# Attention probabilities kept in four places instead of two, with the value products of two chunks issued back to back in every second chunk

## The reference

```python
Q = query @ Wq + bq
K = key @ Wk + bk
V = value @ Wv + bv
scores = jnp.einsum('bhqd,bhkd->bhqk', Q, K) / jnp.sqrt(jnp.float32(HEAD_DIM))
attn = jax.nn.softmax(scores, axis=-1)
ctx = jnp.einsum('bhqk,bhkd->bhqd', attn, V)
```

## Time and profile before

| what | us |
|---|---|
| three timed executions | 533.49, 533.64, 536.86 |
| median | 533.64 |
| span of the profiled execution, first to last instruction | 538.0 |

### The profile page before, as it was taken

One profiled execution on the slowest core, in us unless ns is written; L12 is line 12 of the kernel. 1 busy time (PEld: TensorE's weight loads), 2 busy tenths in 40 slices (PEclk: granted clock), 3 DMA queues, 4 the chain that ended last, 5 costly groups with the idle time before them and its releaser, 6 DMA issues.

```text
span 538.0 us, 10079 instructions
## 1 busy us (share of the span) xinstructions
PE 431.0 (80%) x3977; PEld 249.1 (46%) x3977; DVE 376.2 (70%) x979; ACT 263.5 (49%) x452; POOL 86.3 (16%) x101
## 2 busy tenths in 40 slices
PE   3998877766788878400787899999899899989997
PEld 1344433334556665100233456566566566644444
DVE  7456999999566695885685988889788784271112
ACT  4264888765422393100102456566566567634443
POOL 2000000000100003677891000210210210200000
PEclk9999999989999999755788999999999999999999
DMA  8500266422641202882270003474383382000000
GB/s 287 214 2 0 94 201 186 130 86 86 196 115 57 59 2 66 214 192 85 60 155 18 1 1 76 100 174 94 81 174 78 98 256 60 3 0 1 0 0 17
DMA packets 28718, 50.05 MB, mean 93 GB/s; under 512 B 2464, under 2 KB 18400, under 8 KB 28672
## 3 DMA queue, kind: packets, MB, share of 16 engines
q1 hardware_dynamic: 26848, 45.74, 31.4%
q0 software_dynamic: 1536, 3.67, 2.7%
q10 hardware_dynamic: 288, 0.00, 0.0%
HBM read 39.96 MB, written 9.45 MB: 92 GB/s over the span
## 4 chain that ended last, share of the span: by engine, by line
PE 43%; DVE 37%; issue 8%; POOL 6%; ACT 3%; DMA 2%; DVEq 0%; POOLq 0%
PE banks L1586 7%; PE banks L1562 7%; POOL arena L544 6%; PE banks L1617 5%; DVE arena L1206 5%; DVE mx L1009 4%; DVE work L1235 4%; PE banks L1664 4%; PE banks L1678 4%; DVE arena L1259 2%; PE banks L1292 2%; DVE mx L1017 2%; PE banks L1430 2%; PE banks L1296 2%; DVE work L1201 2%
## 5 line engine op out<-in xcount | busy, mean ns | idle before, releaser
L1009 DVE TENSOR_REDUCE mx<-banks 112x1 f32<-112x500 f32 x168 | 106.9, 675 | 20.2 <-PE banks L1562 20.2
L771 ACT ACTIVATE arena<-banks 128x896 f32<-128x896 f32 x96 | 87.9, 917 | 51.9 <-PE banks L1617 51.2
L1314 PE MATMUL banks<-steps,one 128*128 128x500 f16 (+1 forms) x201 | 56.5, 377 | 32.3 <-DVE hcol L957 32.3
L1586 PE MATMUL banks<-arena 128*32 128x112 f32 (+1 forms) x1536 | 57.3, 265 | 2.9 <-issue 2.0
L1562 PE MATMUL banks<-ctxT,arena 128*112 128x500 bf16 x144 | 54.6, 393 | 5.6 <-issue 1.6
L1586 PEld LDWEIGHTS banks<-arena 128*32 128x32 f32 (+1 forms) x1536 | 33.7, 109 | 24.9 <-issue 20.3
L1235 DVE SCALAR_TENSOR_TENSOR work<-twice,banks,arena 128x202 f32<-128x202 f32 x68 | 29.5, 434 | 19.3 <-PE banks L1430 19.3
L1314 PEld LDWEIGHTS banks<-steps,one 128*128 128x128 f16 x201 | 20.4, 103 | 47.2 <-issue 36.7
L1617 PEld LDWEIGHTS banks<-arena,ctxT 128*128 128x128 bf16 (+1 forms) x576 | 37.3, 104 | 10.5 <-issue 2.8
L1617 PE MATMUL banks<-arena,ctxT 128*128 128x112 bf16 (+1 forms) x576 | 41.1, 213 | 0.6 <-issue 0.6
L544 POOL DMA_INDIRECT arena<-in_w_tab,idx x32 | 33.6, 1051 | 11.6 <-issue 9.4
(11 more groups left out here) (262 smaller groups left out, 751.6 us busy)
## 6 DMA issues: line engine op xcount, KB each, us to landing
ctxT<-key_parts SPq DMA_DIRECT2D x36, 375.0 KB, 6.4
key_parts<-arena SPq DMA_DIRECT2D x32, 281.2 KB, 2.8
ctxT<-in_ctx_T SPq DMA_DIRECT2D x12, 500.0 KB, 8.9
arena<-key_parts SPq DMA_DIRECT2D x12, 375.0 KB, 7.3
ctxT<-in_ctx_nat SPq DMA_DIRECT2D x5, 750.0 KB
arena<-in_ctx_nat SPq DMA_DIRECT2D x3, 750.0 KB
arena<-in_L_ffn_W SPq DMA_DIRECT2D x1, 2048.0 KB, 8.7
arena<-in_fold_w SPq DMA_DIRECT2D x1, 768.0 KB, 5.8
```

The lines of the kernel that those rows point to most:

```text
L771: nc.scalar.activation(Pt[0:rows, g % 2, :].rearrange("p (a n) -> p a n", a=2), banks[0:rows, 2 + 2 * (g % 2):4 + 2 * (g % 2), 0:HQ // 2], ...
L1009: nc.vector.tensor_reduce(mx3[:, b % 2, u // NPIECE, u % NPIECE:u % NPIECE + 1], ps[k % 2][0:2 * NJ, 0:PIECE], AX_X, ALU.max).then_inc(s_m ...
L1314: nc.tensor.matmul(bank[:, 0:cols], one16[:, :], steps16[:, 0:cols], start=True, stop=True, skip_group_check=True)
L1586: last = nc.tensor.matmul(ps[6 + b % 2][q:q + 32, o:o + 2 * NJ], vals[0:rows, v0:v0 + 32], Pt[0:rows, g % 2, 2 * t * NJ:2 * (t + 1) * NJ], ...
```

## The change

The exponentials go to four places instead of two, `g % 4`: the two old ones, one behind the gathered memory rows in the arena, and one in the work buffer. The exponential of chunk g waits for the value product of chunk g-4 instead of g-2. In the loop, value products are issued only in even chunks, two at a time: those of chunks g-2 and g-1. Those of chunks 94 and 95 stand after the loop.

```diff
+        P_RING = 4
+        o_p2 = o_kp + 4 * NHK * 2 * D
+        assert o_p2 + HQ <= o_R + N_R
+        Ps = [Pt[:, 0, :], Pt[:, 1, :], arena[:, o_p2:o_p2 + HQ], later(P, HQ)]
...
-                    if g >= 2:
-                        act.wait_ge(s_pv, g - 1)
+                    if g >= P_RING:
+                        act.wait_ge(s_pv, g - P_RING + 1)
                     nc.scalar.activation(
-                        Pt[0:rows, g % 2, :].rearrange("p (a n) -> p a n", a=2),
+                        Ps[g % P_RING][0:rows, :].rearrange("p (a n) -> p a n", a=2),
...
-                                            Pt[0:rows, g % 2, 2 * t * NJ:2 * (t + 1) * NJ],
+                                            Ps[g % P_RING][0:rows, 2 * t * NJ:2 * (t + 1) * NJ],
...
-                    if g >= 1:
+                    if c % 2 == 0 and g >= 2:
+                        weigh_values(g - 2)
                         weigh_values(g - 1)
...
+            weigh_values(NB * NCH - 2)
             weigh_values(NB * NCH - 1)
```

## The result

The change made the kernel slower: median 541.6 us over 7 runs (540.11 to 544.36) beside 536.86 us of the kernel before in the same comparison, ratio 1.0116 with a 95% interval of 1.0088 to 1.0144 (the quotient of the two medians alone is 1.0088). The forecast was 534.6 us and the range ended at 541.0. Part of that distance is not the change's: the median of before was 533.64 when the forecast was made and is 536.86 here. The change itself was forecast at +1.0 us and measured at +4.7 by the medians, +6.2 by the ratio.

A forecast was written before the change was run, and what follows sets the result against it. The TensorE's own order was taken to bound the loop, DVE close behind. +0.6 (batches 1 to 6), +0.5 (batch 0) and -0.1 (last 14 chunks) gave +1.0 on 533.6: 534.6 us, range 529 to 541.

The forecast's parts named there:

- batch 0: First batch of the attention loop: three plain pairs, the batch end and first pairs paced by DVE, together +0.5 us.
- up to the end of the row units: Batches 1 to 6 of the loop: plain pairs, denominators, reciprocal and batch end, +0.10 us each, +0.6 in all.
- the last 14 chunks: Loop end without row units: pairs slightly longer, one pair with denominators and projection shorter, together -0.1 us.
- Four places, worth nothing: Exponentials waiting for the value product of g-4 start as now; alone worth nothing, it lets products come later.
- The second product at 0.385 us: A value product directly behind another takes 0.385 us instead of 0.52, saving 0.135 per pair of chunks.
- the slower rival: The second product saves nothing: pair 3.19 us, +6.3 us in all, 539.9; chance 0.13.
- The stall: Even chunk's first unit stands 0.33 us for a maximum, 1.19 after the odd one; plain pair 3.05 instead of 2.95.
- The sum of the waits: TensorE waits of units for a maximum, 1.5 us in the loop, should grow by some 6 us.
- Denominators, reciprocal, batch end: Per batch: denominators' matmul between adjacent units -0.22 us, reciprocal delaying the next pair -0.12, release of maxima rows +0.04.
- The tail, +0.07 a pair: In the last 14 chunks a pair takes 2.17 us instead of 2.10, as second products wait for the odd exponential.
- the gaps that no wait explains: 3.6 us of unexplained TensorE idle in the loop, taken as order-independent; all gone 531.0, doubled 538.2; only widens the range.

The follow-up runs named there:

- e1: The changed kernel itself run once more, unaltered, against the kernel before: 542.48 us, ratio 1.0134.

## Why the prediction was wrong

The three conditions side by side, loop in us, show where the time of the change is:

| key-part loads | old order | changed order | difference |
|---|---|---|---|
| at once (before, and e1; the first profile after: 162.2) | 157.9 | 164.4 | 6.5 |
| none | 152.9 | 154.7 | 1.8 |
| spread | 152.9 | 155.2 | 2.3 |

The medians give 4.7 and 7.3 us (the first comparison and the second) with the loads at once, 2.1 without them and 2.5 with them spread. About 2 us are the new rhythm, which the forecast had at +1.0. Split as its sum was, the profiles without loads give +0.7 for batch 0 (forecast +0.5), +1.4 up to the end of the row units (+0.6) and -0.3 for the last 14 chunks (-0.1). The rest, 2.5 us in the first profile after and near 5 in the second, appears only while the loads come at once. In the first it is 1.2 us of longer gaps and 1.3 at low clock.

*Four places, worth nothing: right* (the run with them alone).

*The second product at 0.385 us: right.* Both products and the step to the unit take 0.90 us (352.19 to 353.09), where 0.905 was forecast, and groups start 0.096 us apart across the join too. So the slower rival fell: its sum (539.9) came near the result by luck, as the time was lost by another mechanism. By the rule of the Trainium skill cited for it (TensorE: Matmul & The Clock Gate, "Part 3: Packing small matmuls", The mechanism) these weight loads should not have overlapped; the measurement decides against it here.

*The stall: right in kind, mis-sized.* "The even chunk's first unit needs bank 0 or 1 ..., 1.19 us from unit to unit" and "a unit that has stood needs 0.26 before its scores". It measured 1.28 and 0.23, and the pair 3.11 instead of 3.05. The price was read from chunk 1, whose unit waits for a maximum alone, as the exponential's wait starts only with chunk 2. In every later chunk the first unit carries both. The old order's first units carry both as well and seldom stand, but where one does the price could be read: the unit at 364.98 starts 0.135 us after its maximum is signalled, those of rows 5 0.043. The run with the wait moved gave 1.19 and 3.05. The sum of the waits, "some 6 us" more, was 7.4 for the same reason.

*Denominators, reciprocal, batch end.* The pair at c = 3 and 4 was forecast at 3.17 and is 3.11. The pair that the reciprocal delays was 3.16 and is 3.18 (359.32 to 362.50). From c = 9 to the rows of maxima it was 3.34 and is 3.30 (362.50 to 365.80). A batch, forecast at 0.10 above before, is 0.21 above it in rhythm, and 0.10 below it with the single wait (19.25).

*The tail, +0.07 a pair: wrong in sign, and small.* Two chunks take 2.09 (459.21 to 461.30) where 2.10 was before:

```profile
459.21 0.95 PE L1621 MATMUL banks<-arena,ctxT 128*128 128x112 bf16 x16
460.09 1.27 PE L1590 MATMUL banks<-arena 128*32 128x112 f32 x32
```

*The step that failed* is this: "They depend on neither order that I can see ... They widen the range and decide nothing", of the gaps that no wait explains. The loop of before held 4.2 us of them, which the forecast took as given, with a chance only of their going or doubling by luck. But they changed with every edit, even that of the places alone, which leaves the TensorE's order as it was: issue 4.2 us before, 5.4 and 5.6 after, 2.7 with a wait moved, 0.6 with four places alone, with short maxima 0 in the old order and 5.8 in the changed one. Nor is their length their whole price. Where a gap was 1.45 us the next stretch ran at full clock; behind those of 1.83 and more it ran near half, and the work that followed took up to 1.8 times as long (the two products 1.72 us instead of 0.97). In the first profile after, 5.4 us of gaps and 1.3 at low clock are 6.7 of the 7.5 us by which its loop exceeds the one without loads. In the second, which exceeds it by 9.7, the two stretches at low clock hold some 3.4, set chunk by chunk beside the run without loads.

What the gaps are: that they are caused by the loads is shown, by taking the loads away and by spreading them, in both orders. That they are instructions which arrive late is read from the packets of the instruction queue and was not tested by itself, but the traces leave little room. The loops of the fourteen profiles hold 27 idle pieces that no wait explains, and every one ends 2.4 to 2.9 us after such a packet starts, though the packets lie some 8 us apart. The reverse does not hold: in the old order with short maxima the spacing reached 12.2 us without a gap. The TensorE is the engine that reads so many instructions: 322 matmuls and 322 weight loads in 19.56 us [beside rows 2]. The Trainium skill (Runtime: NRT & Kernel Launch, "Instruction fetch mechanics") says that an engine's instructions come in blocks over a DMA queue of its own and that crossing into the next is mostly hidden. If the gaps are such crossings, it was not hidden beside six loads at once: up to 2.64 us for one of them.

What stays open is why the changed order has the longer gaps. In both traces the TensorE resumed 2.9 us after the late packet (packet at 418.80, work at 421.69; before, 419.33 and 422.19). After the change it had run dry at 419.05, before at 420.74. So it seems to matter where in the stream of instructions the loads catch it, which any edit shifts, and no run fixed that place by itself. The 2.5 to 5 us beyond the rhythm are therefore this program's, not a price of paired products as such: with the loads spread they go. With only the wait moved the loop is still 3.5 us above that of the same order with spread loads (155.9 against 152.4), less than the 5.0 of the old order.

## What to carry to other kernels

Idle time that a profile puts down to nothing is a cost of its own and may not be carried over as a constant: ask what it coincides with, here six loads issued at once, and give it a case on both sides of the forecast. When a unit's delay is priced from one place in the trace, check that the instruction there waits for as many things as the one it stands for; here a second wait on the same matmul cost 0.09 us each time it stood. And compare the stretch that the change touches, not the span: here 3.9 us of slack in an earlier stage hid a loop that was 4.3 us longer.

## What the runs showed of the hardware

- The TensorE stood for pieces of 0.2 to 2.64 us that no wait explains, in a loop of 322 matmuls and 322 weight loads per 19.56 us, while six loads of 375 KB issued together filled the DMA engines. Each piece ended 2.4 to 2.9 us after a packet of the instruction queue started. With the loads issued one per chunk and a half they were gone or down to a single one of 0.6 to 0.8 us (0.9944 for the kernel before, by that alone).
- The clock fell to 1.2 GHz (stretches with granted 0.50 to 0.57) at the end of idle pieces of 1.83, 2.19 and 2.64 us in the middle of the loop or shortly after them, and stayed at 2.4 behind pieces of 1.45 and 1.65 (before) and of 1.76 (changed order with short maxima).
- A row unit with two waits started 0.136 us after the later was signalled, one with a single wait 0.044 after; the wait for the maximum is then an instruction of its own (81 of them, 13 after the other wait was moved).
- Groups of four column-tiled matmuls with different weights followed each other 0.096 us apart, also from one product to the next, though all use all 128 rows.
